# Self-attention values and probabilities as 2-byte halves in a fused decoder layer

## The reference

```python
x = x + attn(layernorm(x), Wq, bq, Wv, bv, anomaly_matrix)
x = x + xattn(layernorm(x), ctx, mask, Wq, Wkv, Wo)        # 4 heads of 64
x = x + ffn(layernorm(x), W1, b1, W2, b2, Wg, bg)          # 4 experts of 1024, top one

def attn(h, Wq, bq, Wv, bv, A):
    norm = ||h||                     # per row
    s = h / (norm + 1e-9)
    q = s @ Wq.T + bq;  v = s @ Wv.T + bv
    probs = softmax(q @ (q @ A).T / sqrt(256))
    return (probs @ v) * norm
```

## Time and profile before

| | us |
|---|---|
| median of 3 runs | 825.46 |
| lowest, highest | 823.55, 825.78 |
| the profiled execution | 823.08 |
| its span, first to last instruction | 821.3 |
| TensorE busy | 759.4 (92%) |
| TensorE weight loads | 684.1 (83%) |
| VectorE busy | 628.6 (77%) |
| ScalarE busy | 457.8 (56%) |
| GpSimd busy | 165.5 (20%) |
| mean granted TensorE clock | 0.977 of full |

### The profile page before, as it was taken

One profiled execution on the slowest core, in us unless ns is written; L12 is line 12 of the kernel. 1 busy time (PEld: TensorE's weight loads), 2 busy tenths in 40 slices (PEclk: granted clock), 3 DMA queues, 4 the chain that ended last, 5 costly groups with the idle time before them and its releaser, 6 DMA issues. The chain is left out here.

```text
span 821.3 us, 19989 instructions
## 1 busy us (share of the span) xinstructions
PE 759.4 (92%) x6226; PEld 684.1 (83%) x6227; DVE 628.6 (77%) x1608; ACT 457.8 (56%) x930; POOL 165.5 (20%) x254
## 2 busy tenths in 40 slices
PE   3978889999999999999999999999998769999996
PEld 2768779989888898888988889888897658999996
DVE  5983747888888888888888888888886755777773
ACT  2544636666666666666666666666664622444342
POOL 3100130212303123031230312303122011222221
PEclk9999999999999999999999999999998959999999
DMA  6232243314223141231412313123169381111110
GB/s 218 72 116 98 72 135 110 103 39 134 65 74 106 38 132 59 80 106 38 132 60 78 106 38 130 63 76 106 38 218 415 123 326 27 36 41 39 40 33 15
DMA packets 51143, 80.90 MB, mean 99 GB/s; under 512 B 4894, under 2 KB 29216, under 8 KB 50976
## 3 DMA queue, kind: packets, MB, share of 16 engines
q1 hardware_dynamic: 49232, 75.63, 27.5%
q0 software_dynamic: 1872, 4.76, 1.6%
HBM read 45.60 MB, written 35.18 MB: 98 GB/s over the span
## 5 line engine op out<-in xcount | busy, mean ns | idle before, releaser
L1134 ACT ACTIVATE ps_cross<-flip 128x512 f16<-128x512 f32 (+1 forms) x256 | 124.8, 515 | 111.2 <-PE flip L846 90.1
L1359 DVE TENSOR_TENSOR ps_cross<-flip,ps_cross 128x512 f16<-128x512 f32 (+1 forms) x256 | 144.9, 583 | 31.6 <-ACT ps_cross L1134 30.0
L1320 ACT ACTIVATE exp_cross<-exp_cross,xneg 128x1024 f32<-128x1024 f32 (+1 forms) x128 | 122.7, 960 | 26.9 <-DVE xneg L1519 26.9
L846 PE MATMUL flip<-ident,exp_cross 128*128 128x128 f32 (+1 forms) x832 | 130.9, 280 | 6.7 <-DVE ps_cross L1359 3.3
L835 PE MATMUL scores<-keys_cross,qt 128*128 128x402 f32 x512 | 125.7, 367 | 2.7 <-ACT exp_self L1309 1.9
L723 PE MATMUL scores<-keys_self,u_tile 128*128 128x512 f32 x384 | 102.4, 404 | 6.3 <-issue 4.6
L846 PEld LDWEIGHTS flip<-ident,exp_cross 128*128 128x128 f32 (+1 forms) x832 | 95.1, 142 | 14.7 <-DVE ps_cross L1359 5.0
L822 PE MATMUL flip<-vals_self,ps_self 128*128 128x256 f32 x768 | 103.0, 288 | 0.0
L857 PE MATMUL cross_out<-vals_cross,ps_cross 128*128 128x128 f16 (+1 forms) x832 | 102.0, 224 | 0.2
L822 PEld LDWEIGHTS flip<-vals_self,ps_self 128*128 128x128 f32 x768 | 96.2, 193 | 0.0
L859 PE MATMUL cross_out<-vals_cross,ps_cross 128*128 128x64 f16 (+1 forms) x832 | 95.2, 195 | 0.0
(11 more groups left out here) (199 smaller groups left out, 1241.8 us busy)
## 6 DMA issues: line engine op xcount, KB each, us to landing
rows_dram<-pads SPq DMA_DIRECT2D x17, 520.0 KB, 3.9
w_piece<-W SPq DMA_DIRECT2D x32, 256.0 KB, 2.9
w_dram<-w_high SPq DMA_DIRECT2D x32, 256.0 KB, 2.3
w_dram<-w_piece SPq DMA_DIRECT2D x32, 256.0 KB, 2.7
w1s<-w_dram SPq DMA_DIRECT2D x8, 1024.0 KB, 13.6
w2s<-w_dram SPq DMA_DIRECT2D x8, 1024.0 KB, 11.4
u_dram<-u_out SPq DMA_DIRECT2D x4, 1024.0 KB, 5.9
u_tile<-u_dram SPq DMA_DIRECT2D x16, 256.0 KB, 2.7
```

Of the source, the lines that this page charges most:

```text
L846: tr = pe.transpose(flip[0:rows, bank(use), n * P:(n + 1) * P], exp_cross[:, h % 2, m * P:m * P + rows], ident[:, :])
L1134: return act.activation(out, in_, ACT.Copy, **kw)
L1320: act.activation(exp_cross[:, h % 2, cols], exp_cross[:, h % 2, cols], ACT.Exp, bias=xneg[:, h % 2, 1:2], scale=-1.0, accum_out=xden[:, ha ...
L1359: return dve.tensor_tensor(out, full, hi, ALU.subtract)
```

## The change

The self attention's values and probabilities become float16. The values are scaled by SELF_TOP over a bound: the Frobenius norm of Wv plus the largest |bv|. VectorE sums the squares of Wv per partition, GpSimd adds over partitions and takes the root, VectorE finishes the bound and its inverse. The probabilities are scaled by P_TOP as they are copied, and both factors are taken back in `norms`, once, at the end of the prologue. `ps_self` gets a fourth buffer, and it and `exp_self` move from the loop's tiles to the tiles that are kept, beside the values (whose size is halved). The loads of b1 and b2 move behind the last load of w2.

```diff
+SELF_TOP = 16384.0
+P_TOP = 16384.0
...
-    vals_self = sb("vals_self", [P, T, 2, D], F32R, keep)
+    vals_self = sb("vals_self", [P, T, 2, D], F16, keep)
+    exp_self = sb("exp_self", [P, N], F32, keep)
+    ps_self = sb("ps_self", [P, 4, 2, 512], F16, keep)
...
-    exp_self = sb("exp_self", [P, N], F32, loop)
-    ps_self = sb("ps_self", [P, 3, 2, 512], F32R, loop)
...
         load_w1(3)
-        sp.dma_start(b1_row[:, :], ...).then_inc(b_loaded, 16)
-        sp.dma_start(b2_row[:, :], ...).then_inc(b_loaded, 16)
         sp.wait_ge(cross_scores_ready, 8 * T)
         for e in range(E - 1):
             load_w2(e)
         sp.wait_ge(cross_p_used, 16 * T)
         load_w2(E - 1)
+        sp.dma_start(b1_row[:, :], ...).then_inc(b_loaded, 16)
+        sp.dma_start(b2_row[:, :], ...).then_inc(b_loaded, 16)
...
         for g in range(4):
+            if g == 1:
+                pool.wait_ge(bound_step, 1)
+                pool.partition_all_reduce(v_bound[:, 1:2], v_bound[:, 0:1], P, bass.bass_isa.ReduceOp.add).then_inc(bound_summed, 1)
+                pool.wait_ge(bound_summed, 1)
+                pool.tensor_tensor(v_bound[:, 2:3], v_bound[:, 1:2], plus_half[:, 0:1], ALU.pow).then_inc(bound_summed, 1)
...
-                    mm = pe.matmul(self_out[:, 0:D], ps_self[:, g % 3, a, n * P:(n + 1) * P], vals_self[:, m, b, :],
+                    mm = pe.matmul(self_out[:, 0:D], ps_self[:, g, a, n * P:(n + 1) * P], vals_self[:, m, b, :],
...
-                copy(vals_self[:, 4 * g + n, 0, :], v_tmp[:, n % 2, :]).then_inc(pro_v_hi, 1)
+                act.wait_ge(self_scale_step, 2)
+                act.activation(vals_self[:, 4 * g + n, 0, :], v_tmp[:, n % 2, :], ACT.Copy,
+                               scale=self_scale[:, 0:1]).then_inc(pro_v_hi, 1)
...
-            if g == 3:
-                act.wait_ge(self_p_used, 4 * j + 1)
-            elif k >= 1:
-                act.wait_ge(self_p_used, 4 * j if g == 0 else 4 * j + g - 3)
-            copy(ps_self[:, g % 3, 0, :], flip[:, bank(("s", g)), :]).then_inc(self_p_hi, 1)
+            if k >= 1:
+                act.wait_ge(self_p_used, 4 * j + g - 3)
+            copy(ps_self[:, g, 0, :], flip[:, bank(("s", g)), :], scale=P_TOP).then_inc(self_p_hi, 1)
...
+                dve.tensor_tensor_reduce(v_tmp..., w_raw[:, 1, :, :]..., w_raw[:, 1, :, :]..., 1.0, 0.0, ALU.mult, ALU.add,
+                                         v_bound[:, 0:1]).then_inc(bound_step, 1)
...
+        dve.tensor_reduce(v_bound[:, 3:4], bv_row[:, :], AX.X, ALU.max, apply_absolute_value=True).then_inc(bound_step, 1)
+        dve.wait_ge(bound_step, 2)
+        dve.wait_ge(bound_summed, 2)
+        dve.tensor_tensor(v_bound[:, 4:5], v_bound[:, 2:3], v_bound[:, 3:4], ALU.add).then_inc(bound_step, 1)
+        dve.wait_ge(bound_step, 3)
+        dve.tensor_scalar(v_bound[:, 5:6], v_bound[:, 4:5], 1e-30, 1.0 / SELF_TOP, ALU.max, ALU.mult).then_inc(bound_step, 1)
+        dve.wait_ge(bound_step, 4)
+        dve.reciprocal(self_scale[:, 0:1], v_bound[:, 5:6]).then_inc(self_scale_step, 1)
+        dve.tensor_scalar(self_scale[:, 1:2], v_bound[:, 5:6], 1.0 / P_TOP, None, ALU.mult).then_inc(self_scale_step, 1)
+        dve.wait_ge(self_scale_step, 2)
...
-                        low(vals_self[:, 4 * g + m, 1, :], v_tmp[:, m % 2, :],
-                            vals_self[:, 4 * g + m, 0, :].bitcast(F32)).then_inc(pro_v_lo, 1)
+                        dve.scalar_tensor_tensor(out=vals_self[:, 4 * g + m, 1, :], in0=v_tmp[:, m % 2, :], scalar=self_scale[:, 0:1],
+                                                 in1=vals_self[:, 4 * g + m, 0, :], op0=ALU.mult, op1=ALU.subtract).then_inc(pro_v_lo, 1)
...
+        dve.wait_ge(norm_step, 16)
+        dve.tensor_scalar(norms[:, :], norms[:, :], self_scale[:, 1:2], None, ALU.mult).then_inc(norm_step, 1)
+        dve.wait_ge(norm_step, 17)
...
-            low(ps_self[:, g % 3, 1, :], flip[:, bank(("s", g)), :], ps_self[:, g % 3, 0, :].bitcast(F32)).then_inc(self_p_lo, 1)
+            dve.scalar_tensor_tensor(out=ps_self[:, g, 1, :], in0=flip[:, bank(("s", g)), :], scalar=P_TOP,
+                                     in1=ps_self[:, g, 0, :], op0=ALU.mult, op1=ALU.subtract).then_inc(self_p_lo, 1)
```

More of the change, by code:

```diff
@@ L109, in emit @@
     v_scale = sb("v_scale", [P, 2], F32)
+    self_scale = sb("self_scale", [P, 2], F32)
     bg_row = sb("bg_row", [P, E], F32)
@@ L162, in emit @@
     v_tmp = sb("v_tmp", [P, 2, D], F32, pro)
+    v_bound = sb("v_bound", [P, 6], F32, pro)
     stats_pro = sb("stats_pro", [P, T, 6], F32, pro)
@@ L261, in emit @@
     pro_v_hi = sem("pro_v_hi")
+    bound_step = sem("bound_step")
+    bound_summed = sem("bound_summed")
+    self_scale_step = sem("self_scale_step")
     pro_v_lo = sem("pro_v_lo")
@@ L548, in _ @@
         load_w1(3)
-        sp.dma_start(b1_row[:, :], bass.AP(io["b1"].tensor, 0, [[0, P], [1, E * DF]])).then_inc(b_loaded, 16)
-        sp.dma_start(b2_row[:, :], bass.AP(io["b2"].tensor, 0, [[0, P], [1, E * D]])).then_inc(b_loaded, 16)
         sp.wait_ge(cross_scores_ready, 8 * T)
@@ L555, in _ @@
         load_w2(E - 1)
+        sp.dma_start(b1_row[:, :], bass.AP(io["b1"].tensor, 0, [[0, P], [1, E * DF]])).then_inc(b_loaded, 16)
+        sp.dma_start(b2_row[:, :], bass.AP(io["b2"].tensor, 0, [[0, P], [1, E * D]])).then_inc(b_loaded, 16)
         sp.wait_ge(spare_stored, 16 * E)
@@ L1410, in _ @@
                 xt_lo_pro(0)
+                dve.tensor_tensor_reduce(v_tmp[:, :, :].rearrange("p c n -> p (c n)"), w_raw[:, 1, :, :].rearrange("p c n -> p (c n)"),
+                                         w_raw[:, 1, :, :].rearrange("p c n -> p (c n)"), 1.0, 0.0, ALU.mult, ALU.add,
+                                         v_bound[:, 0:1]).then_inc(bound_step, 1)
                 statistics_pro(1)
@@ L1436, in _ @@
                         dve.wait_ge(pro_v_biased, 4 * g + m + 1)
-                        low(vals_self[:, 4 * g + m, 1, :], v_tmp[:, m % 2, :],
-                            vals_self[:, 4 * g + m, 0, :].bitcast(F32)).then_inc(pro_v_lo, 1)
+                        dve.scalar_tensor_tensor(out=vals_self[:, 4 * g + m, 1, :], in0=v_tmp[:, m % 2, :], scalar=self_scale[:, 0:1],
+                                                 in1=vals_self[:, 4 * g + m, 0, :], op0=ALU.mult,
+                                                 op1=ALU.subtract).then_inc(pro_v_lo, 1)
             if g < GROUPS - 2:
```

## The result

The changed kernel takes **837.34 us** in the median of 5 runs (834.52 to 838.23), the kernel before 825.46 in 5 runs beside it: ratio 1.014, interval 1.0123 to 1.0157. It is 1.4% slower, where 825.0 was forecast and 829.5 was the end of the range. The profiled execution took 838.23 us, of it a span of 835.8, against 823.08 and 821.3: the span is 14.5 us longer. All 14.5 can be placed by reading the same instruction in both timelines.

A forecast was written before the change was run, and what follows sets the result against it. TensorE was taken to bound the tile loop, VectorE the first part of the prologue. Loop -5.8, prologue +2.9 and bias rows +2.4 sum to -0.5 us, so 825.46 becomes 825.0 us; range 820.5 to 829.5.

The forecast's parts named there:

- The loop: Self-value matmuls with 2-byte operands: 110 ns for 120, 36 of them gain 0.36 us a tile, 5.8 us over 16 tiles.
- The first chain's gain: Tile loop: the first 12 self-value matmuls gain nothing, because the next group waits for VectorE anyway.
- The rival that the type doesn't shorten the stream: Loop: 120 ns belong to 256 columns whatever their width; gain 0 to 2.3 us, total 828.5 to 830.8; chance 0.17.
- my upper end: Prologue: GpSimd's reduction takes at most 3.6 us, making the delay 2.8 instead of 0.65 us; at 0.39 it is hidden.
- rival of a slow reduction: Prologue: GpSimd's reduction over partitions is slow, 2.2 us more, total 827.2; chance 0.15, half of it on the slow side.
- sign of a GpSimd step ending after 17 us: Prologue: a GpSimd step ending after 17 us was listed as showing the forecast wrong.
- the square sum and the chain: Prologue, VectorE: multiply-and-sum of 512 elements, 0.65 us; largest absolute value and four dependent steps ahead of the first keys, 1.2 us.
- 0.8 for the values: Prologue: slower scaled copies and subtractions of values, 0.2 us a pair of tiles, four pairs before the store of u.
- The tail's term: After the last tile: late bias loads delay the last record's landing, so first rows issue 2.4 us later, ends 0 and 3.6.
- my 5.8: Tail: median landing time in us of record writes after 600 us, used for the last record under load; 6.8 at most.
- -0.5: Whole kernel: forecast net change in us, -5.8 loop, +2.9 prologue, +2.4 bias rows.

The follow-up runs named there:

- e3: Changed kernel with the two bias-row loads issued at their old place, an unused tile of 9984 bytes making room; 833.40 us, ratio 1.0115.
- e14: Changed kernel, biases still late, with an unused 96-byte tile so tiles stand 128 bytes further than in the kernel before; 835.60 us, one run.
- e1: Kernel before with only GpSimd's sum over partitions of a constant column added, result unused; 832.95 us beside 824.98, ratio 1.0102.
- e2: Changed kernel with an ordinary GpSimd addition in place of the sum over partitions (result not the layer's); 829.85 us, ratio 1.0061.
- e8: Changed kernel without the bound, constants as scales, biases at the old place, tiles 128 bytes further than before; 821.72 us beside 826.36, ratio 0.9942.
- e10: Kernel before with only the bias-row loads moved behind the last w2; 830.71 us beside 825.80, ratio 1.0059; repeated once, 827.83 us.
- e15: Changed kernel with 120 instead of 76 filler transposes on TensorE ahead of the feed-forward part; 835.79 us, one run.
- e5: Changed kernel with the sum over partitions done by a TensorE matmul against ones, copied out by VectorE; 832.14 us beside 826.36, ratio 1.0065.
- e6: Changed kernel with the sum on TensorE, biases loaded at the old place, tiles 128 bytes further than before; 826.26 us beside 826.36, ratio 0.9994.
- e9: Same as e6, but TensorE's sum stands between the first two query chains and VectorE copies it earlier; 825.26 us beside 825.80, ratio 0.9998.
- e4: Changed kernel with an unused tile of 32 bytes a partition behind the new scale tile; 839.06 us, one run.
- e12: From e6: ScalarE squares and sums the weights and copies TensorE's sum, GpSimd finishes most of the bound in ordinary operations; 823.22 us beside 826.12, ratio 0.9971.
- e13: Kernel before with an unused tile moving all tiles behind it by 64 bytes; 825.54 us, one run.

## Why the prediction was wrong

**The loop was right.** Forecast 0.36 us a tile; measured 0.35 (34.23 to 33.88), and 4.4 us over the twelve steps from tile 3 to 15, 4.3 by the forecast. A value matmul went from 120 to 109.6 ns (forecast 110), and 36 of them make 0.37 us, so nothing is left for the fourth buffer, which had no run of its own. The first chain's gain went into the wait for VectorE: for the self flips it rose from 1.5 to 3.9 us over the run, and at flip 3 by 0.2 to 0.3 us a tile, as forecast. Both operands of these matmuls became 2-byte, and their weight loads went from 193 to 99 ns too; which of the two gives the shorter step is not shown. The rival that the type doesn't shorten the stream is refuted. Its rule in the Trainium skill (TensorE: Matmul & The Clock Gate, Back-to-back issue gap), which the page states for isolated matmuls and without a type, makes 109.2 ns for 256 columns: the trace agrees for 2 bytes and not for 4. Of the 5.8 us, 5.0 are seen from tile 3 to the end of attention. The first tiles gave nothing that can be told: from first scores to tile 3 the profiles of before's kind take 93.2 to 96.6 us and those of the changed kind 93.5 to 95.1.

**The step that failed is in the prologue:** "GpSimd gets a reduction over partitions and a power between 14.9 and 17.0, where it is idle. The trace shows such a reduction as 0.39 us ... so 3.6 is the upper end." I priced the operation and not the way to it. The row itself, carries "41.10" of idle time ahead of it, so anything up to 41 us could be hidden there, and my upper end came from the 3.6 us behind the row only. The view of that source line of before has the sign too:

```profile
L622 POOLq MODIFY_POOL_CONFIG  x2: 7/7/7, 40.7 to 40.8; - x2
```

a change of configuration 41 us before the reduction, in time that nobody needed. In the seven profiles with a reduction where the changed kernel has it, 7.7 to 10.2 us went by from that change of configuration to the reduction, and 6.7 to 7.7 on the way back. In the two shortest, e3 (8.3) and e14 (7.7), the row sums came 1.2 to 1.4 us later and were what the reduction waited for last, so the way there was done by then. The run paid 8.0 us in e1; of q to w it is 8.7 there and, from the other side, 9.0 in e2. My rival of a slow reduction named the right place, with 2.2 us more; its size rested on the same upper end, and my sign of a GpSimd step ending after 17 us came true. The Trainium skill states the kind of cost (GPSIMD Engine Reference, Instruction dispatch): the first call to a freshly loaded kernel of GpSimd pays about 6 us more, with no instruction to be seen. By that page's figure, as an estimate: counted from the row sums at 14.9 it would end the reduction at 21.3, 2.8 us beyond my upper end; counted from 8.5, where the change of configuration was issued, it would be hidden. The changed kernel's trace has 10.0 us for the way there, and a way back besides.

The other terms of the prologue were right, which the runs show one by one: 0.65 + 1.2 = 1.85 for the square sum and the chain, 1.83 measured (54.06 in e2 less 52.23 in e8); 0.8 for the values, 0.9 measured (e8 less before), both good to some 0.3 us. 51.37 + 0.9 + 1.8 + 9.0 is the changed kernel's 63.07; these steps are differences from one run to the next, so they add up in any case, and what tests the 9.0 is e1's 8.7.

**The tail's term was mis-sized, and lacked a part.** "2.4 us later. Ends: 0 ... 3.6": the rows came 3.95 us later, since the landing took 7.1 us under the biases and not my 5.8. The mechanism was the one named (e3, e10). What had no term is TensorE: the earlier trace rows end where the fillers still ran, and I did not ask how long they last. They end 3.6 us too early for rows 4 us later, the granted clock behind that is 0.68, and 1.3 us are lost (e15 has 1.00, and 1.0 us of it back).

**The tile of 8 bytes** had no term either: 0.9 us.

The sum with the measured sizes, against the span: -5.0 (loop) + 1.7 (first tiles) + 11.6 (prologue) + 3.95 + 1.3 + 0.9 = 14.5. With my own terms and only the 9.0, 1.6, 1.3 and 0.9 added, -0.5 would have been +12.3, 837.8 for a measured 837.3.

**Still open:** why e5, e6 and e9 take 34.0 us a tile where the changed kernel, e2, e3, e4, e8, e12, e14 and e15 take 33.9, which is 1.5 to 1.8 us over the twelve steps; what ran the first tiles slower in the changed kernel's profile; and the mechanism behind the place of the tiles.

## What to carry to other kernels

An operation's row prices the operation and not the way to it: read the idle time ahead of it and behind it, and what the queue issued there, before it is moved to a place where the engine is needed within microseconds. On GpSimd the way to a sum over partitions and back took 15 to 17 us, once for a row of such operations, so put it where nothing is asked for as long, or add over partitions with a 128x1 matmul against ones. A load moved behind a stream delays every landing that a later step waits for, and the filler that keeps TensorE's clock up has to be made longer with the wait.

## What the runs showed that I had not expected

- GpSimd went over to the reduction as soon as the ordinary operation ahead was done, 6 us before its input was there. The other operations queued on it waited all the same.
- Second-layer matmuls with 4-byte operands took 113.5 or 118 ns by the place of the tiles modulo 128 bytes: 143.1 us for the feed-forward part at 64 bytes (e13) against 141.7 at 0.
- A stretch of 66 matmuls in the same program took 8.4, 9.8 or 11.0 us, at a granted clock of 1.00, 0.82 and 0.72; single profiles differ by as much as 3 us ahead of the steady tiles, more than several of the effects under study.
